# First attention: the addition of a group's sums moves from the end of its step on VectorE to behind the next step's first addition of counts

## The chip, the cores and the metric

One core of one Trainium2 chip runs the whole program. The time is the device time of one execution in microseconds; three runs of the kernel before gave 2632.73, 2643.93 and 2664.64 us. The profile is of one further execution. A core has the engines TensorE (PE, its weight loads PEld), VectorE (DVE), ScalarE (ACT), GpSimd (POOL) and SyncE (SP), which run their own instruction streams and wait for each other by semaphores.

## What is computed

A graph network of four layers over 3125 nodes and 100000 edges, the edges sorted by destination, each layer followed by a residual layer norm. The change touches the first layer, an attention with 4 heads of 16 features:

```python
score = (Kh[src] * Qh[dst] * (1.0 / np.sqrt(D)) * Ee).sum(-1)
score = jnp.exp(jnp.clip(score, -5.0, 5.0))
msg = Vh[src] * score[..., None]
wV = jax.ops.segment_sum(msg, dst, num_segments=n)
```

`Ee` is a linear map of 64 edge attributes. Beside it the same loop counts, for the second layer, how many edges go from each source to each destination.

## The kernel before, in words

The edges are worked in G = 98 groups of 1024 (128 partitions by C = 8 tiles). Every engine runs its own loop over the groups, unrolled by RS = 4, since the ring of gathered rows `kv`, of edge attributes `ea`, of indices `idx` and of query windows `qwin` has four slots. `j` counts sweeps over the edges; one sweep is run here.

GpSimd (L472 to L480) gathers keys and values of a group's sources by eight indirect DMAs (L476), one for each tile, into slot s of `kv`. After the fifth gather of a group it waits for the next group's indices, so it works in bursts: three gathers that finish one group and five of the next. SyncE (L423 to L433) waits on the semaphore `slot_free` until group g-4 is added, and then loads the indices (L338, 4 KB) and the edge attributes (L433, 256 KB) of group g.

VectorE's `step` (L627 to L673) for group g, in order: `prod` = edge products (bank 3, awaited by `ee_ok`) times gathered keys (L641); load of five registers of the group from `base_i` (L643: place `b` of the window of sums, and four places of the counts); times the query products (bank 4, `qd_ok`, L649); sum over the head's features (L651); clip (L653), which releases ScalarE's exponential; the first addition of counts (`add_counts(0)`, L635); the one-hot columns of the next group's nodes (`node_hots`, L613); the second addition of counts; the messages (L662, awaiting `ex_ok`); the third and fourth additions of counts; the key columns of the next group (`key_hots`, eight instructions at L620); and last the group's sums, bank 5 into `acc` (L672), awaiting `sum_ok`, with `slot_free` raised by it. That last one is what the change moves.

TensorE's `step` (L867 to L894): two of the four counts of the group (L875, two matmuls each; each waits for its bank by `bank_free`, raised by VectorE's additions), the turning of the next group's edge attributes (L833), the other two counts, the turning of its node columns (L841), the sums of the group (L890, awaiting `msg_ok`, raising `sum_ok`), and then the next group's edge products (L850, L852, raising `ee_ok`) and query products (L858, raising `qd_ok`).

ScalarE's `step` (L749 to L753): the exponential (L751), then for the next group: wait for `slot_free` of an earlier group, two loads of the query window (L733), copies of the turned edge attributes (L735) and node columns (L737), and the columns for the counts (L741, L747).

`pipelined` (L341 to L349) writes the loop: `front` of group 0, a hardware loop of 24 rounds of four steps from 0, and the last two groups behind it.

Of the kernel before, what the change touches and what calls it, by code (L numbers as in the profile page):

```python
# [8 lines left out]
ALU, ACT, AX = mybir.AluOpType, mybir.ActivationFunctionType, mybir.AxisListType  # L9

P = 128
N, D, E = 3125, 64, 100000
# [6 lines left out]
G = -(-E // ST)  # L19
PL = (E - (G - 1) * ST) // C  # L20
W = 64
# [3 lines left out]
GG = C // GT  # L25
# [3 lines left out]
RS = 4  # L29
# [37 lines left out]
def build(nc, x, src, dst, edge_attr_2, edge_attr_64, Wq, bq, Wk, bk, We, be, Wv, bv,  # L67
          attn_w, W_fc, W_attn, W_edge, W_e2n, W_m1, W_m2, out):
    ctx = ExitStack()
    with ctx:  # L70
# [50 lines left out]
        base_i = sb("base_i", [1, G, 8], i32)  # L121
# [252 lines left out]
        with nc.Block() as block:  # L374
# [115 lines left out]
            def _(dve):  # L490
# [115 lines left out]
                with dve.Fori(0, nj) as j:  # L606
                    dve.wait_ge(cleared, j + 1)
                    pass_on(dve)
                    start_sweep(dve, begun, True)

                    def node_hots(g, s, m):

                        nc.vector.tensor_tensor(hots[:, s % 2, :, :], bc(dst_rel[:, bass.ds(g, 1), :].rearrange("p g c -> p (g c)"), 2, W),  # L613
                                                bc(iota[:, 0:W], 1, C), ALU.is_equal).then_inc(hot_ok, 1)

                    def key_hots(g, s, m):

                        keys = tile_key[:, bass.ds(g, 1), :].rearrange("p g c -> p (g c)")
                        for c in range(C):
                            last = nc.vector.tensor_scalar(key_hot[:, c, :], iota_key[:, :], keys[:, c:c + 1], None, ALU.is_equal)  # L620
                        last.then_inc(key_ok, 1)

                    def front(g, s, m):
                        node_hots(g, s, m)
                        key_hots(g, s, m)

                    def step(g, s, m, after):  # L627

                        n = j * G + g + 1

                        def add_counts(q):

                            at = count[:, :, bass.ds(group_at[q], WC)]
                            dve.wait_ge(count_ok, j * (G * GG) + g * GG + q + 1)
                            nc.vector.tensor_tensor(at, at, bank[6 + q % 2][:, 0:KC].rearrange("p (h w) -> p h w", w=WC),  # L635
                                                    ALU.add).then_inc(bank_free, 1)

                        kvs = kv[:, s, :, :]
                        dve.wait_ge(kv_in[s], m * (16 * C))
                        dve.wait_ge(ee_ok, n)  # L640
                        nc.vector.tensor_tensor(prod[:, :].rearrange("p (c f) -> p c f", c=C),  # L641
                                                bank[3][:, :].rearrange("p (c f) -> p c f", c=C), kvs[:, :, 0:D], ALU.mult)
                        b, *group_at = nc.values_load_multi_w_load_instructions(  # L643
                            base_i[0:1, bass.ds(g, 1), 0:1 + GG].rearrange("a g k -> a (g k)"), engines=[mybir.EngineType.DVE],
                            min_val=0, max_val=NP,
                            skip_runtime_bounds_check_because="start_sweep keeps them within 0 and NP")[1]
                        dve.drain()
                        dve.wait_ge(qd_ok, n)
                        nc.vector.tensor_tensor(prod[:, :], prod[:, :], bank[4][:, :], ALU.mult)  # L649
                        dve.drain()  # L650
                        nc.vector.tensor_reduce(score[:, :], prod[:, :].rearrange("p (a d) -> p a d", d=DH), AX.X, ALU.add)  # L651
                        dve.drain()
                        nc.vector.tensor_scalar(score[:, :], score[:, :], -5.0, 5.0, ALU.max, ALU.min).then_inc(sc_ok, 1)  # L653

                        add_counts(0)
                        if after:

                            node_hots(*after)
                        dve.drain()
                        add_counts(1)  # L660
                        dve.wait_ge(ex_ok, n)
                        nc.vector.tensor_tensor(msg[:, :, 0:D].rearrange("p c (h d) -> p c h d", h=H),  # L662
                                                kvs[:, :, D:2 * D].rearrange("p c (h d) -> p c h d", h=H),
                                                bc(expo[:, :].rearrange("p (c h) -> p c h", h=H), 3, DH), ALU.mult).then_inc(msg_ok, 1)
                        for q in range(2, GG):
                            dve.drain()
                            add_counts(q)
                        if after:

                            key_hots(*after)  # L670
                        dve.wait_ge(sum_ok, n)
                        nc.vector.tensor_tensor(acc[0:D + 1, bass.ds(b, W)], acc[0:D + 1, bass.ds(b, W)], bank[5][0:D + 1, 0:W], ALU.add).then_inc(slot_free, 1)  # L672
                        dve.drain()  # L673

                    pipelined(dve, front, step)

            @block.scalar
            def _(act):
# [2501 lines left out]
```

## Time and the profile before

| | us |
|---|---|
| median of three runs | 2643.93 |
| the profiled execution | 2622.77 |
| its span, first to last instruction | 2621.0 |
| VectorE busy in the span | 1421.5 (54%) |
| GpSimd busy in the span | 1243.5 (47%) |
| TensorE matmuls busy in the span | 1481.0 (57%) |

A row of a group of instructions reads: line, engine, operation, out<-in, shapes, count | busy time in us, mean ns of one | idle time of the engine just before them in us, and what ended most of it. A row of a timeline reads: start in us from the span's start, duration in us, engine, line, operation, tiles, shape, count, and in brackets the idle time before it with what released it. "Issue" is time in which the engine waited for nothing that the profile shows; "remote" names no engine. Starts of matmuls are recorded, their ends are modelled. The first attention's loop runs from about 60 to 1466 us of the span.

### The profile page before, as it was taken

The page shows a single profiled execution, that of the slowest core. Times are in us where ns is not written, and L with a number is a line of the kernel's source. Part 1 is how long each engine was busy: PE and PEld are TensorE (multiplying, and loading weights), DVE is VectorE, ACT ScalarE, POOL GpSimd, SP SyncE. Part 2 cuts the span into 40 slices and gives each one's busy share as a digit, 9 for nine tenths or more (in the row PEclk, how much of TensorE's full clock was granted, in tenths as well). Part 3 has the DMA queues.
Part 4 walks back from the last instruction along what each step waited for, and adds up shares of the span by engine and source line. Part 5 has one row for each costly group of instructions (what it writes and reads, how often), then busy time and mean ns, then how long its engine had stood idle before and what let it go on. Part 6 is the DMA issues. An engine that isn't in the chain of part 4 may idle for free. (4 is left out here: it accounts for less than half of the span.)

```text
span 2621.0 us, 43664 instructions
## 1 busy us (share of the span) xinstructions
PE 1481.0 (57%) x12911; PEld 1234.8 (47%) x12911; DVE 1421.5 (54%) x3789; ACT 1011.9 (39%) x2229; POOL 1243.5 (47%) x1346
## 2 busy tenths in 40 slices
PE   4555555555555555555454586586103655556697
PEld 4444443434443443444343486475103645455586
DVE  6555554555555555555454787886202534344586
ACT  4333333333333333333233490591103533344575
POOL 5455555555555555555455191273764343444300
PEclk7777777777777777777777698696556777777898
DMA  4222222222222222222122120004111111111110
GB/s 130 52 58 58 56 59 54 60 57 57 58 58 58 55 59 58 58 57 56 52 59 55 39 67 22 1 2 125 35 24 25 36 34 38 34 42 32 35 34 14
DMA packets 112819, 128.69 MB, mean 49 GB/s; under 512 B 68447, under 2 KB 75923, under 8 KB 112426
## 3 DMA queue, kind: packets, MB, share of 16 engines
q0 software_dynamic: 35776, 62.74, 10.2%
q1 hardware_dynamic: 54842, 59.37, 7.8%
q10 hardware_dynamic: 22064, 4.85, 0.9%
q8 instruction: 75, 1.23, 0.2%
q14 instruction: 62, 0.51, 0.1%
HBM read 116.64 MB, written 10.20 MB: 48 GB/s over the span
## 5 line engine op out<-in xcount | busy, mean ns | idle before, releaser
L476 POOL DMA_INDIRECT shared<-kv_tab,idx x784 | 756.5, 965 | 668.0 <-DMA idx<-in_src 435.5
L875 PE MATMUL bank<-key_hot,lo_hot 128*128 128x350 f16 x784 | 218.7, 391 | 593.9 <-DVE count L635 399.1
L875 PEld LDWEIGHTS bank<-key_hot,lo_hot 128*128 128x128 f16 x784 | 57.5, 100 | 711.3 <-issue 699.2
L2455 POOL DMA_INDIRECT count<-att_tab,count x240 | 232.6, 969 | 261.4 <-PE bank L3009 156.0
L672 DVE TENSOR_TENSOR acc<-acc,bank 65x64 f32 x98 | 21.3, 218 | 486.2 <-remote 485.6
L751 ACT ACTIVATE expo<-score 128x32 f32<-128x32 f32 x98 | 22.5, 229 | 616.5 <-DVE score L653 609.9
L2837 ACT ACTIVATE shared<-shared 128x126 f32<-128x126 bf16 x336 | 143.6, 484 | 279.2 <-remote 175.6
L635 DVE TENSOR_TENSOR count<-count,bank 128x350 f32 x392 | 205.2, 523 | 81.6 <-issue 73.9
L741 ACT ACTIVATE lo_dist<-iota_neg,tile_lo 128x128 f16<-128x128 f32 x784 | 238.4, 390 | 0.0
L2986 PE MATMUL bank<-shared 128*128 128x150 f32 x896 | 156.7, 319 | 121.6 <-issue 56.2
L2986 PEld LDWEIGHTS bank<-shared 128*128 128x128 f32 x896 | 138.8, 208 | 146.2 <-issue 137.8
L620 DVE TENSOR_SCALAR key_hot<-iota_key,tile_key 128x350 f16<-128x350 f16 x784 | 192.3, 317 | 0.0
L890 PEld LDWEIGHTS bank<-hots,msg 128*65 128x65 f32 x1568 | 184.8, 222 | 0.4 <-DVE msg L662 0.4
L890 PE MATMUL bank<-hots,msg 128*65 128x64 f32 x1568 | 181.2, 304 | 0.0
L2952 PE MATMUL bank<-shared,ad_row 128*128 128x25 bf16 x1344 | 64.9, 177 | 205.5 <-issue 205.4
L2692 DVE TENSOR_TENSOR count<-count,bank 128x500 f32 x112 | 74.9, 668 | 167.6 <-remote 141.8
L2952 PEld LDWEIGHTS bank<-shared,ad_row 128*128 128x128 bf16 x1344 | 51.5, 99 | 216.2 <-issue 215.3
L850 PE MATMUL bank<-webd,eaT 128*128 128x128 f32 x784 | 144.0, 342 | 0.9 <-issue 0.9
L3020 PE MATMUL bank<-count,tab 128*68 128x88 f32 x1400 | 134.8, 265 | 8.4 <-DVE count L2692 6.5
L2455 POOL DMA_INDIRECT g_edge<-att_tab,count x94 | 88.9, 946 | 98.2 <-PE bank L3009 70.8
L3020 PEld LDWEIGHTS bank<-count,tab 128*68 128x68 f32 x1400 | 129.7, 162 | 12.2 <-DVE count L2692 8.6
L850 PEld LDWEIGHTS bank<-webd,eaT 128*128 128x128 f32 x784 | 132.4, 255 | 1.3 <-issue 1.3
(539 smaller groups left out, 3235.6 us busy)
## 6 DMA issues: line engine op xcount, KB each, us to landing
shared<-in_edge_attr SPq DMA_DIRECT2D x97, 256.0 KB
shared<-lo_tab SPq DMA_DIRECT2D x28, 512.0 KB
shared<-kv_tab,idx POOLq DMA_INDIRECT x784
count<-att_tab,count POOLq DMA_INDIRECT x240
qwin<-q_tab ACTq DMA_DIRECT2D x196, 16.0 KB
g_edge<-att_tab,count POOLq DMA_INDIRECT x94
idx<-in_src SPq DMA_DIRECT2D x93, 4.0 KB, 1.5
dh_tab<-acc SPq DMA_DIRECT2D x1, 1176.0 KB
```

The costliest lines, as they stand in the source:

```text
L476: nc.gpsimd.indirect_dma_start(kv[:, s, c, :], None, kv_tab, bass.IndirectOffsetOnAxis(ap=of[:, s, c:c + 1], axis=0)).then_inc(kv_in[s], 16)
L620: last = nc.vector.tensor_scalar(key_hot[:, c, :], iota_key[:, :], keys[:, c:c + 1], None, ALU.is_equal)
L635: nc.vector.tensor_tensor(at, at, bank[6 + q % 2][:, 0:KC].rearrange("p (h w) -> p h w", w=WC), ALU.add).then_inc(bank_free, 1)
L741: nc.scalar.activation(lo_dist[:, c, :], iota_neg[:, :], ACT.Abs, bias=los[:, c:c + 1])
L850: nc.tensor.matmul(bank[3][:, q * P:(q + 1) * P], eaT[:, q * P:(q + 1) * P], webd[:, :], start=q == 0, stop=False, skip_group_check=True)
L875: last = nc.tensor.matmul(bank[6 + q % 2][:, 0:KC], lo_hot[:, c, :], key_hot[:, c, :], start=i == 0, stop=i == GT - 1)
L890: last = nc.tensor.matmul(bank[5][0:D + 1, 0:W], msg[:, c, :], hots[:, s % 2, c, :], start=c == 0, stop=c == C - 1)
L2455: nc.gpsimd.indirect_dma_start(ring[s][:, j, 0:D + 2], None, att_tab[1], bass.IndirectOffsetOnAxis(ap=src_i[:, t:t + 1], axis=0)).then_inc ...
L2837: nc.scalar.activation(low_w[:, n % LOW_RING, 0:FREE], low_dist[:, n % LOW_RING, 0:FREE], ACT.Relu, bias=p, scale=minus_p).then_inc(low_ok, 1)
L2952: last = nc.tensor.matmul(bank[0][:, t * NT:(t + 1) * NT], lo_turned[:, s, t, :], u_parts[:, k, :], start=k == 0, stop=k == 2)
L2986: nc.tensor.matmul(into[:, 0:NT * QW].rearrange("p (h w) -> p h w", w=QW)[:, :, bass.ds(at[j], TW)], low_w[:, n % LOW_RING, :], keys_w[:, ...
L3020: last = nc.tensor.matmul(sum_of[0:D + 4, 0:UW], tab[:, h, 0:D + 4], blocks[:, i % 2, h, :], start=h == 0, stop=h == NT - 1, skip_group_ch ...
```

## The change

VectorE's stream alone is changed. `add_sums(g, s)` loads the window's place `b` by itself, waits for `sum_ok`, adds, and raises `slot_free`. It is called for group g-1 in the step of group g, behind `add_counts(0)`; the last group adds its own at the end of its step. The step's register load takes four registers in place of five. Since group 0 has none before it, the loop is written out: four steps peeled, then 23 rounds of four, then the last two.

```diff
+                    def add_sums(g, s):
+
+                        b = spans(dve, g)
+                        dve.wait_ge(sum_ok, j * G + g + 1)
+                        nc.vector.tensor_tensor(acc[0:D + 1, bass.ds(b, W)], acc[0:D + 1, bass.ds(b, W)], bank[5][0:D + 1, 0:W], ALU.add).then_inc(slot_free, 1)
+
                     def step(g, s, m, after):
 
                         n = j * G + g + 1
+                        first = isinstance(g, int) and g == 0
...
-                        b, *group_at = nc.values_load_multi_w_load_instructions(
-                            base_i[0:1, bass.ds(g, 1), 0:1 + GG].rearrange("a g k -> a (g k)"), engines=[mybir.EngineType.DVE],
+                        group_at = nc.values_load_multi_w_load_instructions(
+                            base_i[0:1, bass.ds(g, 1), 1:1 + GG].rearrange("a g k -> a (g k)"), engines=[mybir.EngineType.DVE],
...
                         add_counts(0)
+                        if not first:
+                            add_sums(g - 1, (s - 1) % RS)
                         if after:
 
                             node_hots(*after)
...
                             key_hots(*after)
-                        dve.wait_ge(sum_ok, n)
-                        nc.vector.tensor_tensor(acc[0:D + 1, bass.ds(b, W)], acc[0:D + 1, bass.ds(b, W)], bank[5][0:D + 1, 0:W], ALU.add).then_inc(slot_free, 1)
+                        else:
+                            add_sums(g, s)
                         dve.drain()
 
-                    pipelined(dve, front, step)
+                    front(0, 0, 1)
+                    for g in range(RS):
+                        step(g, g, 1, (g + 1, (g + 1) % RS, (g + 1) // RS + 1))
+                    with dve.Fori(1, G // RS) as it:
+                        for s in range(RS):
+                            step(it * RS + s, s, it + 1, (it * RS + s + 1, (s + 1) % RS, it + 1 + (s + 1) // RS))
+                    for g in range(G - G % RS, G):
+                        step(g, g % RS, g // RS + 1, (g + 1, (g + 1) % RS, (g + 1) // RS + 1) if g + 1 < G else None)
```

## Rows read from the trace of the kernel before

**Rows 1.** The page's costliest groups: GpSimd's gathers and the addition of the sums.
```profile
L476 POOL DMA_INDIRECT shared<-kv_tab,idx x784 | 756.5, 965 | 668.0 <-DMA idx<-in_src 435.5
...
L672 DVE TENSOR_TENSOR acc<-acc,bank 65x64 f32 x98 | 21.3, 218 | 486.2 <-remote 485.6
```

**Rows 2.** Who waited for whom, 60 to 1467 us: total us, times, longest us.
```profile
SPq L325 <- DVE acc L672: 1229.7, 93, 24.3
...
DVE acc L672 <- remote: 485.6, 93, 7.3
```

**Rows 3.** One group in order of time, all engines, 715 to 730 us.
```profile
715.27 0.22 DVE L672 TENSOR_TENSOR acc<-acc,bank 65x64 f32 x1 [4.83 <-remote]
715.68 0.69 DVE L641 TENSOR_TENSOR prod<-bank,shared 128x512 f32<-128x512 f32 x1 [0.19 <-issue]
...
716.47 0.69 DVE L649 TENSOR_TENSOR prod<-prod,bank 128x512 f32<-128x512 f32 x1
...
718.01 0.94 POOL L476 DMA_INDIRECT shared<-kv_tab,idx  x1 [4.49 <-DMA idx<-in_src]
...
718.27 0.52 DVE L635 TENSOR_TENSOR count<-count,bank 128x350 f32 x1
718.71 0.68 DVE L613 TENSOR_TENSOR hots<-dst_rel,iota 128x512 f32<-128x512 f32 x1
...
719.64 0.52 DVE L635 TENSOR_TENSOR count<-count,bank 128x350 f32 x1 [0.25 <-issue]
...
720.85 1.06 PE L841 MATMUL bank<-ident,hots 128*128 128x128 f32 x4
...
721.70 1.65 PE L890 MATMUL bank<-hots,msg 128*65 128x64 f32 x16
...
721.94 0.60 ACT L737 ACTIVATE hotT<-bank 128x512 f32<-128x512 f32 x1 [1.18 <-issue]
...
724.23 0.38 PE L852 MATMUL bank<-be_parts,ones_b 3*128 3x512 bf16 x1
...
724.55 1.16 PE L858 MATMUL bank<-qwin,hotT 128*128 128x128 f32 x8
...
726.68 0.76 PE L875 MATMUL bank<-key_hot,lo_hot 128*128 128x350 f16 x4 [0.98 <-ACT lo_hot L747]
726.95 0.94 POOL L476 DMA_INDIRECT shared<-kv_tab,idx  x1 [0.30 <-issue]
...
729.50 0.22 DVE L672 TENSOR_TENSOR acc<-acc,bank 65x64 f32 x1 [5.27 <-remote]
```

**Rows 4.** VectorE in order of time, 1230 to 1266 us.
```profile
1230.96 0.22 DVE L672 TENSOR_TENSOR acc<-acc,bank 65x64 f32 x1 [4.87 <-remote]
...
1242.14 0.22 DVE L672 TENSOR_TENSOR acc<-acc,bank 65x64 f32 x1 [2.22 <-remote]
1249.83 0.69 DVE L641 TENSOR_TENSOR prod<-bank,shared 128x512 f32<-128x512 f32 x1 [7.47 <-remote]
1257.52 0.69 DVE L649 TENSOR_TENSOR prod<-prod,bank 128x512 f32<-128x512 f32 x1 [7.00 <-remote]
...
1265.05 0.21 DVE L672 TENSOR_TENSOR acc<-acc,bank 65x64 f32 x1
```

**Rows 5.** GpSimd, first and last of sixteen gathers, 1230 to 1260 us.
```profile
1234.63 1.27 POOL L476 DMA_INDIRECT shared<-kv_tab,idx  x1 [5.44 <-DMA idx<-in_src]
...
1253.88 0.94 POOL L476 DMA_INDIRECT shared<-kv_tab,idx  x1 [0.30 <-issue]
```

**Rows 6.** TensorE's edge and query products in the same stretch.
```profile
1239.80 0.39 PE L852 MATMUL bank<-be_parts,ones_b 3*128 3x512 bf16 x1
1240.11 1.16 PE L858 MATMUL bank<-qwin,hotT 128*128 128x128 f32 x8
```

**Rows 7.** VectorE behind the last gather, 1448 to 1460 us.
```profile
1448.87 0.21 DVE L672 TENSOR_TENSOR acc<-acc,bank 65x64 f32 x1
...
1459.11 0.21 DVE L672 TENSOR_TENSOR acc<-acc,bank 65x64 f32 x1
```

## The prediction

> **What bounds the kernel now.** I read the page's costliest groups first, then who waited for whom, then one group in order of time. On the page GpSimd's gathers (L476, 784 of them) are the largest busy time, and nearly as long again idle, most of it until indices land; VectorE's addition of the sums (L672) has the longest idle time in front of it of all VectorE groups [rows 1]. The waits say the same as a ring: SyncE waits for L672 in 93 groups, and L672 waits 93 times, 485.6 us in all or 5.22 each, for something "remote" [rows 2]. "Remote" is put where the releasing semaphore moved long after the engine that should have moved it had ended.
>
> One group shows the ring closed [rows 3]. L672 at 715.27 frees the slot; the first gather of a burst of eight starts at 718.01 (2.74 later, the loads of indices between); the eighth starts at 726.95 and takes 0.94, so the burst lasts 9.88; the next L672 starts 1.61 after its end, at 729.50. 2.74 + 9.88 + 1.61 = 14.23 us, and that is the period. The point is the last term. The sums' products (L890) are drawn as ended at 721.70 + 1.65 = 723.35 and VectorE was through with the key columns at 724.23, but L672 starts at 729.50: after 5.27 of idle time, and 1.61 after the burst. So here a completion of TensorE that falls into a burst of gathers reaches VectorE only when the burst is over. Is it the sums' alone? Two groups in which GpSimd ran on without a pause answer it [rows 4 to 6]: a burst went from 1234.63 to 1254.82 (sixteen gathers), and there VectorE waited not only for the sums (1242.14) but then 7.47 us for the edge products (L641, whose last matmul L852 is drawn as ended at 1240.19) and 7.00 for the query products (L649; L858 ended at 1241.27). So the hold takes TensorE's later results too, and in a long burst lets them through one after another, over 7 us apart. In the common group they are late as well but behind L672: they cost nothing of their own. Without gathers, at the end, the period is 1459.11 - 1448.87 = 10.24 us [rows 7]: that is VectorE's and TensorE's own chain. GpSimd's least is eight gathers at the step of that burst, 8 x (726.95 - 718.01) / 7 = 10.2 us.
>
> When does the hold begin? In rows 3 the transposes L841, drawn to 720.85 + 1.06 = 721.91, 3.9 us into the burst, were in time (ScalarE's copy L737 follows at 721.94), the sums, drawn to 5.3 us in, were not.
>
> The Trainium skill says otherwise ("SBUF - State Buffer", Who interferes with whom): DMA never contends with a compute engine, and only VectorE and GpSimd can block each other, at the shared port. By that rule the gathers cannot be what holds TensorE's results; the rows above go against it, and what it would make of the time is the last rival.
>
> **The change part by part.**
> 1. *The wait leaves the end of the step.* From group 0 on VectorE goes from L620 straight to L641. Removed there: L672's 0.22 and its issue gap, 715.68 - 715.27 = 0.41 [rows 3]. Late next is L641's own input, the edge products. In the present cadence they are not released before the sums, so at this place the change alone gains 0.41 at most.
> 2. *The sums are added behind the first count.* L641 to the first L635 is 718.27 - 715.68 = 2.59 [rows 3]. Behind L635 comes L672 at a spacing of at least 0.44 (L613 followed so), plus the register load of the window's place, which now stands here. The trace of before has no such load in this position: between 0 (hidden under L635's 0.52) and about 0.25 (the issue gap ahead of the second L635, 719.64, where a register is worked out behind a drain). I take 0.60 from L635 to L672. L613 and everything behind it comes later by about as much: 0.60 against 0.44 and L672's 0.22, say 0.5 to 0.6.
> 3. *What is queued behind it.* The slot is freed by L672, so SyncE's two loads and GpSimd's burst move with it: 2.59 + 0.60 = 3.19 us later against L641, 3.34 behind the first count. ScalarE waits for slots of three groups earlier and is not reached. No DMA is added; their order is the same.
> 4. *The peeled first four groups* and the last addition: more code, run once; a microsecond or two, unseen.
>
> Now the results of TensorE against the new burst. Taken from rows 3, counted from the first L635 (718.27) and 0.60 later than now, the burst starting at 3.34: sums end at 5.08 + 0.60 = 5.68, that is 2.3 into the burst; edge products (724.61) at 6.94, 3.6 in; query products (725.71) at 8.04, 4.7 in; the first counts (727.44) at 9.77, 6.4 in. The hold began between 3.9 and 5.3 in. So sums and edge products would pass, the query products stand on the edge and the counts behind it. I take the query products as held: the sixteen matmuls of the sums, within which the hold began in rows 3, now lie in the burst's first 2.3 us, and should bring it on no later than they did. Then L649 starts where L672 started before, 1.61 after the burst, and the new period is
> 1.61 + (L649 to first L635, 718.27 - 716.47 = 1.80) + 0.60 + 2.74 + 9.88 = 16.63 us, 2.40 more.
> If the edge products are held too, L641 is the one released and it is 1.61 + 2.59 + 0.60 + 2.74 + 9.88 = 17.42, 3.19 more. The two groups of the long burst, where exactly these products were held, took 1265.05 - 1230.96 = 34.09, 17.05 each [rows 4]: between the two.
> Of 93 waits of L672 two belong to that odd pair; 91 periods x 2.40 = +218 us. The profiled execution took 2622.8 us around a span of 2621.0; the median of the runs is 2643.9, 0.8% above it. On the execution the sum gives 2841, on the median 2862. The spread of the three runs is 1.2%, so about 1% is what a measurement can tell from no change.
>
> **The rivals.**
> *Only the counts are held (0.14).* The query products pass, the counts don't: 1.61 + 0.60 + 2.74 + 9.88 = 14.83, +0.60 x 91 = +55: 2699. For it: 4.7 lies in a window of 3.9 to 5.3. Against: with the products in time and a few counts let through one by one, the slot comes free inside the burst, which then runs on as in rows 5.
> *Only the sums are late (0.08).* Then L641 and L649 go ahead, VectorE stands at L672 behind the first count, and it is released where it is now: 1.61 + 2.74 + 9.88, the ring is the same, +0: 2644. It would also mean that the change removes a wait and finds it again a few instructions on. Against it: rows 4, where L641 and L649 wait 7 us each.
> *The burst comes too late to hold anything that matters (0.22), the faster side.* The slot is freed later, the burst starts later against TensorE's work; if the hold begins more than 4.7 us into a burst for the query products, and more than 6.4 for the counts, then the next step starts unheld. The bound is the tail's 10.24 [rows 7] or GpSimd's 10.2. But the slots then come free while a burst runs, GpSimd no longer pauses, and rows 4 and 5 show what an unbroken burst costs. Half of the way from 14.23 to 10.24, 2.0 x 91 = -182: 2462. It decides at 4.7 us: hold later than that, faster; earlier, slower.
> *No hold by gathers at all (0.06).* The wait of L672 would be the sums' own delay of some other cause, covered by the new place; the period is that of the tail, 3.99 x 91 = -363: 2281. Rows 4 speak against it, and the idle time of L672, which is there only while gathers run (rows 7 have none). By the rule of the Trainium skill cited above this is the case to expect.
>
> **How the numbers follow.** Forecast 0.50: 2862, its own range 2750 (products let through after part of the burst) to 2950 (edge products held: 2644 + 290 = 2934). Slower by over 1%: 0.50 and 0.10 of the first rival, 0.60. Within 1%: 0.04 of it and 0.08, 0.12. Faster by over 1%: 0.22 + 0.06 = 0.28. The range for eight in ten reaches from 2400, past the faster rival's 2462, to 2950; left out are the last rival and some 0.05 on either side.
>
> **What would show it.** Right: L672 directly behind the first L635 with next to no idle time; the idle time of 5.2 us has moved to L649 (or L641), "remote"; the bursts still of eight gathers with a pause, the pause longer than now (about 6.8 us against 14.23 - 9.88 = 4.35), the period 16.6 to 17.4; SyncE still waiting for L672 in every group. Wrong: L672 waits at its new place and the period is 14.2 (sums alone); or L641, L649 and L672 all without idle time and a period near 10 to 12 (the faster side); or bursts of sixteen, short and long groups in turn, which would give a mean I can't place better than between the cases.

## The result, and the profile after the change

The changed kernel takes 2879.5 us (median of 4 runs, 2871.7 to 2892.3) against 2654.3 for the kernel before in the same measurement (4 runs, 2632.7 to 2665.6). The ratio is 1.086, with a 95% interval of 1.077 to 1.096: slower. The forecast was 2862 with a range of 2750 to 2950, and the measured time lies 17 above the one and inside the other. Every time in us below is read from one profiled execution of its kernel; that of e2 took 2801.7 us, slower than its other four runs (2743.6 to 2755.5).

The profiled execution took 2885.2 us (span 2883.4). Its page, the groups that answer to [rows 1]:

```profile
L476 POOL DMA_INDIRECT shared<-kv_tab,idx x784 | 752.8, 960 | 911.3 <-DMA idx<-in_src 676.8
...
L648 DVE TENSOR_TENSOR prod<-bank,shared 128x512 f32<-128x512 f32 x98 | 67.8, 692 | 557.8 <-remote 510.7
...
L656 DVE TENSOR_TENSOR prod<-prod,bank 128x512 f32<-128x512 f32 x98 | 67.5, 688 | 231.7 <-remote 229.6
```

The gathers cost what they did (752.8 us busy against 756.5), but GpSimd stands idle in front of them for 911.3 us instead of 668.0. The addition of the sums (now L631) is not among the costliest groups any more. The idle time marked "remote" now stands ahead of the edge products' multiplication (L648) and the query products' (L656), 740.3 us together against the 485.6 of the sums before. The waits, 60 to 1750 us (us in total, times, longest), beside [rows 2]:

```profile
SPq L325 <- DVE acc L631: 1447.1, 92, 27.4
POOL shared L476 <- DMA idx<-in_src: 676.8, 94, 18.6
DVE prod L648 <- remote: 510.7, 87, 8.7
DVE prod L656 <- remote: 229.6, 95, 5.7
```

One group in order of time, all engines, 711 to 732 us (start, duration, engine, line; idle time before in brackets), beside [rows 3]:

```profile
711.85 0.22 DVE L631 TENSOR_TENSOR acc<-acc,bank 65x64 f32 x1
...
714.81 0.95 POOL L476 DMA_INDIRECT shared<-kv_tab,idx  x1 [7.04 <-DMA idx<-in_src]
715.00 1.96 PE L906 MATMUL bank<-hots,msg 128*65 128x64 f32 x16
...
717.93 0.38 PE L868 MATMUL bank<-be_parts,ones_b 3*128 3x512 bf16 x1
718.24 1.16 PE L874 MATMUL bank<-qwin,hotT 128*128 128x128 f32 x8
...
723.46 0.69 DVE L648 TENSOR_TENSOR prod<-bank,shared 128x512 f32<-128x512 f32 x1 [6.07 <-remote]
723.65 0.94 POOL L476 DMA_INDIRECT shared<-kv_tab,idx  x1 [0.30 <-issue]
726.34 0.69 DVE L656 TENSOR_TENSOR prod<-prod,bank 128x512 f32<-128x512 f32 x1 [2.19 <-remote]
...
728.15 0.53 DVE L642 TENSOR_TENSOR count<-count,bank 128x350 f32 x1
728.71 0.22 DVE L631 TENSOR_TENSOR acc<-acc,bank 65x64 f32 x1
...
731.77 0.95 POOL L476 DMA_INDIRECT shared<-kv_tab,idx  x1 [7.17 <-DMA idx<-in_src]
```

Read it as a ring again. The addition at 711.85 frees the slot; the burst starts at 714.81 (2.96 later) and its eighth gather ends at 723.65 + 0.94 = 724.59 (9.78); the query products, drawn as ended at 718.24 + 1.16 = 719.40, reach VectorE at 726.34 (1.75 behind the burst); 1.81 to the first count, 0.56 to the addition. 2.96 + 9.78 + 1.75 + 1.81 + 0.56 = 16.86 us. The addition itself has no idle time before it, as the prediction asked for; the bursts are still of eight gathers (93 of the 95), the pause between them is 7.04 and 7.17 us here against the 6.8 forecast, and SyncE still waits for the addition, 92 times. TensorE's own speed is not in this ring: its granted clock in the group was 0.70 against 0.77 from 700 to 730 us before, but the query products are drawn as ended 6.94 us before VectorE gets them. Over the whole stage the first and the last of the 98 additions start at 93.20 and 1706.90, 16.64 us a group; before it was 82.96 and 1466.11, 14.26 a group. So the last addition comes 240.8 us later. The two spans differ by 262.4; the other 21.6 us lie behind the stage (2883.4 - 1706.9 = 1176.5 us against 1154.9). They are scatter: in e3 and e8 below, which have the same code there, that part took 1153.9 and 1148.2, and in e1 1179.0.

### The profile page after: what moved, and what is told of

Same layout as the page of the kernel before. It is cut to its first block and busy times, and to the rows that moved or that the text cites. A ratio compares the mean times of both kernels' runs of the same rounds, so it can differ in the third digit from the quotient of the medians.

```text
span 2883.4 us, 43835 instructions
## 1 busy us (share of the span) xinstructions
PE 1531.2 (53%) x12911; PEld 1292.2 (45%) x12911; DVE 1415.4 (49%) x3789; ACT 1013.4 (35%) x2229; POOL 1237.9 (43%) x1346
## 5 line engine op out<-in xcount | busy, mean ns | idle before, releaser
L476 POOL DMA_INDIRECT shared<-kv_tab,idx x784 | 752.8, 960 | 911.3 <-DMA idx<-in_src 676.8
L891 PE MATMUL bank<-key_hot,lo_hot 128*128 128x350 f16 x784 | 225.1, 401 | 823.6 <-DVE count L642 799.0
L648 DVE TENSOR_TENSOR prod<-bank,shared 128x512 f32<-128x512 f32 x98 | 67.8, 692 | 557.8 <-remote 510.7
L906 PEld LDWEIGHTS bank<-hots,msg 128*65 128x65 f32 x1568 | 192.4, 230 | 0.4 <-DVE msg L671 0.4
L906 PE MATMUL bank<-hots,msg 128*65 128x64 f32 x1568 | 189.8, 313 | 0.0
L656 DVE TENSOR_TENSOR prod<-prod,bank 128x512 f32<-128x512 f32 x98 | 67.5, 688 | 231.7 <-remote 229.6
L866 PE MATMUL bank<-webd,eaT 128*128 128x128 f32 x784 | 167.8, 382 | 0.9 <-issue 0.9
L866 PEld LDWEIGHTS bank<-webd,eaT 128*128 128x128 f32 x784 | 154.4, 292 | 1.3 <-issue 1.3
```

The costliest lines, as they stand in the source:

```text
L476: nc.gpsimd.indirect_dma_start(kv[:, s, c, :], None, kv_tab, bass.IndirectOffsetOnAxis(ap=of[:, s, c:c + 1], axis=0)).then_inc(kv_in[s], 16)
L866: nc.tensor.matmul(bank[3][:, q * P:(q + 1) * P], eaT[:, q * P:(q + 1) * P], webd[:, :], start=q == 0, stop=False, skip_group_check=True)
L891: last = nc.tensor.matmul(bank[6 + q % 2][:, 0:KC], lo_hot[:, c, :], key_hot[:, c, :], start=i == 0, stop=i == GT - 1)
L906: last = nc.tensor.matmul(bank[5][0:D + 1, 0:W], msg[:, c, :], hots[:, s % 2, c, :], start=c == 0, stop=c == C - 1)
```

## The experiments

Twelve kernels ran. Each is compared by its ratio to the kernel before in the same measurement, because the kernel before took 2608 to 2614 us there and not 2654. "Period" is the time from the first to the last of the 98 additions of sums in the kernel's own trace, divided by 97.

| Run | What is different | Ratio (95% interval) | Period, us |
|---|---|---|---|
| kernel before | | 1 | 14.26 |
| changed kernel | | 1.086 (1.077 to 1.096) | 16.64 |
| e1 | written-out loop, sums at end | 0.994 (0.990 to 0.998) | 13.82 |
| e2 | slot freed behind messages | 1.054 (1.052 to 1.056) | 15.66 |
| e3 | slot freed at end of step | 1.098 (1.094 to 1.103) | 16.57 |
| e4 | changed, 4 gathers | 0.923 (0.918 to 0.927) | 12.05 |
| e5 | changed, plain loads | 0.839 (0.832 to 0.845) | 9.91 |
| e6 | before, sums of 2 tiles | 1.067 (1.059 to 1.075) | 15.95 |
| e7 | before, waits for 5 and 3 | 0.992 (0.988 to 0.996) | 13.89 |
| e8 | changed, waits for 5 and 3 | 1.087 (1.078 to 1.095) | 16.24 |
| e9 | before, plain loads | 0.811 (0.806 to 0.816) | 9.14 |
| e10 | before, 4 gathers | 0.822 (0.815 to 0.829) | 9.38 |
| e11 | before, burst started by TensorE's sums | 0.931 (0.923 to 0.938) | 12.25 |
| e12 | before, pause after every 4 gathers | 1.008 (1.004 to 1.012) | 14.45 |

### e1: the written-out loop alone

```diff
                         add_counts(0)
-                        if not first:
-                            add_sums(g - 1, (s - 1) % RS)
...
                             key_hots(*after)
-                        else:
-                            add_sums(g, s)
+                        add_sums(g, s)
```

> The loop written out as in the changed kernel, the sums still added at the end of the step (with the register load that the new function brings). Theory (the place of the addition makes the difference, by way of the slot that it frees): the ring is that of before, one group every 14.2 us, ratio to the kernel before 0.99 to 1.01. Rival (the written-out code or the second register load costs something by itself): some part of the 0.086, so a ratio over 1.02.

Measured: 2602.3 us, ratio 0.994 (0.990 to 0.998). As the theory said; the loop written out and the second register load cost nothing, and if anything give 12 us back. By the traces it is 13.82 us a group against 14.26, so against this kernel the place of the addition costs 2.82 us a group and not 2.38. What follows is about that place.

### e2 and e3: another instruction frees the slot

Both keep the sums where the changed kernel has them and take the semaphore from the addition. e2 gives it to the drain behind the messages, e3 to the last drain of the step.

```diff
-  ... bank[5][0:D + 1, 0:W], ALU.add).then_inc(slot_free, 1)
+  ... bank[5][0:D + 1, 0:W], ALU.add)
...
                         for q in range(2, GG):
-                            dve.drain()
+                            d = dve.drain()
+                            if q == 2:
+                                d.then_inc(slot_free, 1)
```

> The changed kernel, but the slot is freed by the first drain behind the messages and no longer by the addition of sums. The burst of gathers then starts some 6 us behind the first count instead of 3.5. Theory (what counts is which of TensorE's results fall late into the burst): edge and query products of the next group fall 1 to 2.5 us into the burst and go through, the later counts or the sums are held; the idle time leaves the edge and query products, and the period falls below 16.9, to 14 to 16 us: ratio to the kernel before 0.99 to 1.07. Rival 1 (each microsecond by which the slot is freed later makes the period one microsecond longer, whatever falls where): 16.9 + 2.6 = 19.5 us, ratio near 1.17. Rival 2 (the place of the addition matters by itself, not the slot): 16.9 us as in the changed kernel, ratio 1.09.

> The changed kernel, but the slot is freed by the drain at the end of the step, some 6 us behind the first count, so the burst starts some 8.7 us behind it. Theory: next group's products and its first count lie ahead of the burst or early in it and go through; what is late in the burst are that group's messages' counts and sums, and the slot of the next group comes free while the burst still runs, so bursts run into each other. Between the kernel before and the changed one: period 14 to 17 us, ratio 0.99 to 1.09. Rival 1 (one microsecond of slot is one of period): 16.9 + 5.4 = 22.3 us, ratio about 1.27. Rival 2 (place of the addition by itself): ratio 1.09.

Measured: e2 2753.7 us, ratio 1.054; e3 2861.5 us, ratio 1.098 (1.094 to 1.103), a little above the theory's 1.09. e2 frees the slot later than the changed kernel and is faster all the same: that refutes "a microsecond of slot is a microsecond of period" as well as "the place of the addition by itself". e3 is far from that rival's 1.27. A stretch of e2 in order of time, all engines:

```profile
807.21 0.69 DVE L648 TENSOR_TENSOR prod<-bank,shared 128x512 f32<-128x512 f32 x1 [11.64 <-remote]
...
815.60 1.07 POOL L476 DMA_INDIRECT shared<-kv_tab,idx  x1 [11.37 <-DMA idx<-in_src]
...
817.33 0.69 DVE L648 TENSOR_TENSOR prod<-bank,shared 128x512 f32<-128x512 f32 x1 [1.03 <-PE bank L870]
...
822.61 0.46 PE L893 MATMUL bank<-key_hot,lo_hot 128*128 128x350 f16 x2 [1.20 <-DVE count L642]
822.93 1.08 PE L859 MATMUL bank<-ident,hots 128*128 128x128 f32 x4
...
824.13 0.52 DVE L642 TENSOR_TENSOR count<-count,bank 128x350 f32 x1 [0.25 <-issue]
...
828.42 0.60 ACT L755 ACTIVATE hotT<-bank 128x512 f32<-128x512 f32 x1 [5.46 <-remote]
...
830.51 0.37 PE L876 MATMUL bank<-qwin,hotT 128*128 128x128 f32 x1 [0.24 <-issue]
...
832.64 0.37 PE L876 MATMUL bank<-qwin,hotT 128*128 128x128 f32 x1 [1.76 <-issue]
...
838.54 0.69 DVE L648 TENSOR_TENSOR prod<-bank,shared 128x512 f32<-128x512 f32 x1 [11.96 <-remote]
```

The groups come in pairs. In the first the products (817.33) lie 1.7 us into the burst and go through. So does all of that group's work up to its last count: TensorE's (L893) is drawn as ended 7.5 us into the burst, and VectorE adds it at 824.13 without a "remote" wait. Then the slot comes free inside the burst, GpSimd runs on, and the next group is caught: the transposes drawn to 822.93 + 1.08 = 824.01 reach ScalarE's copy at 828.42, TensorE's own instructions go out one every 2.1 us (830.51, 832.64), and the edge products arrive at 838.54 after 11.96 us of idle time. The pair takes 838.54 - 807.21 = 31.3 us. So e2's ratio came as its theory said, but the idle time left the edge products only in every second group: 478.4 us "remote" at L648 are left, in 47 waits. e3 has such pairs too, slower: its L648 stands idle 14.66 us "remote" (829.59) and 1.39 us (840.30) in turn. Its bursts here are of eight with 1.24 us between two of them, and that gap (816.56 to 817.79) did not let the edge products through, which are drawn as ended at 815.79. This is the pattern that the prediction named for bursts of sixteen, and what it gave as the case against its faster rival [rows 4, 5].

### e4 and e10: half the gathers, in both orders

```diff
                        for c in range(C):
-                            nc.gpsimd.indirect_dma_start(
+                            if c < C // 2:
+                              nc.gpsimd.indirect_dma_start(
...
-                        dve.wait_ge(kv_in[s], m * (16 * C))
+                        dve.wait_ge(s_const, 5)
+                        dve.wait_ge(kv_in[s], m * (16 * C // 2))
```

`s_const` is raised once, ahead of the stage, when GpSimd has filled the other half of the slots with zeros.

> The changed kernel with four gathers in a group instead of eight: the key and value rows of tiles 4 to 7 are left out (zeros in their place), everything else stands. The burst lasts about 4.9 us instead of 9.8. Theory (the gathers hold TensorE's completions till the burst is over): either nothing is held, and the period is VectorE's own, 10.2 to 10.6 us, or the query products, drawn 4.6 us into the burst, are held to 1.75 behind it: 1.75 + 1.81 + 0.56 + 2.96 + 4.9 = 12.0 us. 2880 - 91 x 4.9 = 2435 or, without any hold, 2290 us; ratio to the kernel before 0.86 to 0.92. Rival (TensorE's results are late for a reason that has nothing to do with gathers): idle time ahead of the products stays, period 16.9 or little less, ratio over 1.05.

> The kernel before with four gathers in a group instead of eight, as in e4 (key and value rows of tiles 4 to 7 left out). Burst from 2.7 to 7.7 us behind the addition of sums. Theory: the sums are drawn as ended 8.1 us behind it, after the burst, so nothing is held that matters, and the period is VectorE's own, 10.2 to 10.5 us against 12.2 in e4: ratio 0.85 to 0.87, e4 0.06 to 0.07 slower than this. Rival (the later addition hurts by other ways than the hold, or the hold catches counts here): period over 11 us, ratio over 0.88.

Measured: e4 2403.1 us, ratio 0.923; e10 2142.8 us, ratio 0.822. e4 in order of time, VectorE and GpSimd:

```profile
808.27 0.22 DVE L633 TENSOR_TENSOR acc<-acc,bank 65x64 f32 x1
...
811.20 0.95 POOL L478 DMA_INDIRECT shared<-kv_tab,idx  x1 [7.43 <-DMA idx<-in_src]
...
815.03 0.94 POOL L478 DMA_INDIRECT shared<-kv_tab,idx  x1 [0.30 <-issue]
...
816.92 0.69 DVE L651 TENSOR_TENSOR prod<-bank,shared 128x512 f32<-128x512 f32 x1 [3.01 <-remote]
...
820.43 0.22 DVE L633 TENSOR_TENSOR acc<-acc,bank 65x64 f32 x1
```

With the burst 5 us shorter the wait moves with its end: released 0.95 us behind the last gather (816.92 against 815.97), group 12.2 us, where the theory's held case said 12.0. That the two lie so close is partly luck: the theory had the query products held, to 1.75 behind the burst, and here it is the edge products, to 0.95, with 2.95 us from them to the first count and not 1.81. In 30 of the 98 groups the same wait ends on the edge products without a "remote". In e10 nothing is held, and one group follows the other in 8.9 to 9.4 us. The ratios of the two orders differ by 0.923 - 0.822 = 0.10. That is more than the 0.06 to 0.07 I had expected, because e10 is faster than the 10.2 us that I had taken for VectorE's own chain.

### e5 and e9: no gathers, plain loads of the same bytes

```diff
+                        for c in range(C):
+                            sp.dma_start(kv[:, s, c, :], kv_tab[c * P:(c + 1) * P, :]).then_inc(kv_in[s], 16)
...
-                            nc.gpsimd.indirect_dma_start(
-                                kv[:, s, c, :], None, kv_tab, bass.IndirectOffsetOnAxis(ap=of[:, s, c:c + 1], axis=0)
-                            ).then_inc(kv_in[s], 16)
```

> The changed kernel without gathers: SyncE loads eight blocks of 128 consecutive rows of the key and value table into the same places of the slot, the same number of bytes and of rows; the rows are not those that the edges name, so the attention is computed from other keys and values. GpSimd has nothing left to do in the stage. Theory (GpSimd's gathers hold TensorE's completions): nothing is held, the period is VectorE's and TensorE's own of 10.2 to 10.6 us, the kernel near 2270 to 2320 us, ratio to the kernel before 0.86 to 0.88. Rival (it is the traffic into SBUF, whoever issues it): results late in the load are still released behind its end, idle time marked remote ahead of the products, period over 11.5 us, ratio over 0.91.

> The kernel before with the plain loads of e5 in place of its gathers (the key and value rows are again not those of the edges). With e5 it makes the fourth corner: both places of the addition, with gathers and without. Theory (the place of the addition costs only through the gathers that it starts): the same as e5 within 1%, period 10.0 to 10.3 us, ratio to the kernel before 0.83 to 0.85. Rival (the two places differ by themselves): the later place saves a wait or costs one without gathers too, over 1% between the two; the part of it that is the changed kernel's 0.086 would show as a ratio near 0.77 here.

Measured: e5 2197.0 us, ratio 0.839; e9 2118.8 us, ratio 0.811. The same stretch of VectorE's addition in e5 and then in e9:

```profile
799.87 0.22 DVE L633 TENSOR_TENSOR acc<-acc,bank 65x64 f32 x1
...
809.93 0.22 DVE L633 TENSOR_TENSOR acc<-acc,bank 65x64 f32 x1
```

```profile
800.75 0.21 DVE L674 TENSOR_TENSOR acc<-acc,bank 65x64 f32 x1
...
810.06 0.21 DVE L674 TENSOR_TENSOR acc<-acc,bank 65x64 f32 x1
```

In neither does VectorE wait once for anything "remote" in this stage. The changed kernel falls from 16.64 to 9.91 us a group: it is the gathers, and not the 0.5 MB of traffic into the same slot, that hold TensorE's results. But the theory's "same within 1%" fell. The changed order takes 0.839 / 0.811 = 1.034 times as long even here, 0.77 us a group. In e9 the addition stands behind the key columns, while TensorE works on sums and edge products; in e5 it stands ahead of the messages (VectorE from L650 to L673: 811.45 - 806.41 = 5.04 us; in e9 from L643 to L664 806.14 - 801.70 = 4.44), on which TensorE's sums wait, and these on which the next edge products. That is 0.60 us here and 0.64 in the mean of the stage; half of the 0.64 is the addition, the other 0.31 a longer way from the edge products' multiplication to the query products', where VectorE waits for TensorE (0.47 us ahead of L658 in this group of e5). For the rest there is the granted clock of TensorE, in the stretch from 200 to 700 us (busy time of the engines, then PEclk, DMA share, GB/s; e5, then e9):

```profile
200.00:700.00 500.00, 351.38 (x2459) 277.09 (x2457) 379.99 (x956) 245.37 (x601) 0.00 (x0) 0.87 0.30 82
```

```profile
200.00:700.00 500.00, 347.50 (x2679) 265.58 (x2678) 405.31 (x1040) 268.60 (x659) 0.00 (x0) 0.93 0.33 90
```

0.87 against 0.93. Whether the lower clock is cause or effect of the longer group these runs don't tell.

Is it TensorE's code that comes late, fetched behind the gathers? Between 200 and 1200 us of the changed kernel's trace the instruction queues moved 4 packets in all, in some sixty groups, nearly all of which were held: no.

### e6: fewer of TensorE's instructions

```diff
-                        for c in range(C):
-                            last = nc.tensor.matmul(bank[5][0:D + 1, 0:W], msg[:, c, :], hots[:, s % 2, c, :], start=c == 0, stop=c == C - 1)
+                        for c in range(2):
+                            last = nc.tensor.matmul(bank[5][0:D + 1, 0:W], msg[:, c, :], hots[:, s % 2, c, :], start=c == 0, stop=c == 1)
```

> The kernel before, the sums of a group taken over two of its eight tiles: 4 of TensorE's 16 instructions of the sums are left, and the sums of the other six tiles are left out. Everything else stands. In e2 TensorE's results passed until 8 us into a burst and the hold began with the sums again, so it may come from the number of TensorE's instructions, the sums' being the densest run of them. Theory A (the hold builds up with TensorE's instructions inside a burst): with 12 fewer the sums pass, and of what follows perhaps the edge and query products too; the wait of the sums' addition falls from 5 us to under 1, and the period to 10.5 to 12.5 us, ratio 0.87 to 0.94. Theory B (it begins a fixed time into the burst, 4 to 5 us): the sums, ended 1.2 us earlier, may pass, but edge and query products at 5.0 and 6.1 us in are held; their wait takes the place of the sums', period 14 to 17 us, ratio 0.99 to 1.09.

Measured: 2787.2 us, ratio 1.067 (1.059 to 1.075). Theory A's forecast (0.87 to 0.94) fell, theory B's time came; a build-up by TensorE's instructions is not excluded by that, since the edge products bring their own. VectorE, e6:

```profile
810.48 0.20 DVE L672 TENSOR_TENSOR acc<-acc,bank 65x64 f32 x1
...
822.89 0.69 DVE L641 TENSOR_TENSOR prod<-bank,shared 128x512 f32<-128x512 f32 x1 [12.22 <-remote]
825.75 0.69 DVE L649 TENSOR_TENSOR prod<-prod,bank 128x512 f32<-128x512 f32 x1 [2.16 <-remote]
```

With the sums smaller, they are through in time (no idle time at 810.48), the slot comes free inside the burst, the next burst joins on, and the edge products wait 12.22 us. GpSimd in the same stretch, the first and last of sixteen gathers:

```profile
802.98 0.94 POOL L476 DMA_INDIRECT shared<-kv_tab,idx  x1 [12.89 <-DMA idx<-in_src]
...
822.02 0.94 POOL L476 DMA_INDIRECT shared<-kv_tab,idx  x1 [0.30 <-issue]
```

To take TensorE work away made the kernel 7% slower: this is the trap of the faster rival, by another door.

### e7 and e8: two waits meant to split the burst

```diff
                         for c in range(C):
+                            if g >= RS and c in (0, 5):
+                                pool.wait_ge(qd_ok if c == 0 else sum_ok, j * G + g - 2)
+                                pass_on(pool)
                             nc.gpsimd.indirect_dma_start(
```

> The kernel before, with each group's gathers in two bursts: gathers 0 to 4 wait until TensorE has given the query products of three groups before, gathers 5 to 7 until it has given that group's sums. e4 showed results released 0.95 us behind the last of four gathers. Theory (a pause in the gathers lets through what is held): from query products to sums 5 x 1.25 + 0.95 = 7.2 us, from sums to the next query products 3 x 1.25 + 0.95 = 4.7 us, period 11.9 to 12.9 us: 2614 - 91 x (14.2 - 12.4) = 2450, ratio to the kernel before 0.91 to 0.95. Rival (the hold lasts as long as any gather is queued, or the two waits cost more than they give): 14.2 us or more, ratio 1.00 to 1.10.

> The same two bursts in the changed kernel. Theory (the place of the addition hurts only by the place of the burst that it starts): the slot is asked for long after it came free, so both orders of VectorE give the same within 0.3 us a group, ratio 0.91 to 0.95. Rival (the later addition costs by itself): its 2.6 us a group remain, ratio 0.09 above that of e7.

Measured: e7 2594.7 us, ratio 0.992; e8 2835.5 us, ratio 1.087. Neither the gain nor the equality of the orders. The two kernels are what e1 and the changed kernel were, and the traces show why: GpSimd still runs bursts of eight (in e7 805.77 to 816.18) and still waits for indices, 392.3 us in 93 waits (e1: 371.1 in 94). My waits were the last to pass once at most (2.3 us "remote" in e7, 0.3 in e8). The code puts the wait for the next group's indices ahead of gather 5 of a group, so a burst is gathers 5 to 7 of one group and 0 to 4 of the next, and both begin only when the same sums have freed a slot. A flaw of the experiment; it says nothing on pauses. e12 and e11 put it right.

### e11: TensorE's sums start the burst

```diff
                         for c in range(C):
+                            if c == 5 and g >= RS - 1:
+                                pool.wait_ge(sum_ok, j * G + g - 2)
+                                pass_on(pool)
                             nc.gpsimd.indirect_dma_start(
...
-                            if c == C // 2 and RS <= g + 1 < G:
+                            if c == C - 1 and RS <= g + 1 < G:
                                 indices(g + 1)
```

> The kernel before; a burst of eight is started by TensorE's completion of the sums itself: gathers 5 to 7 of a group, whose slot is long free, wait for it, and only gathers 0 to 4 of the next group wait for the indices, which land meanwhile. That takes the 2.7 us between the addition and the first gather out of the ring. Theory, if the transposes and counts still pass, now 2.5 us later in the burst: 9.9 + 1.6 + 0.3 = 11.8 us, ratio 0.91 to 0.93. Rival (they are held too, as the hold in e2 and e3 began between 5 and 8 us into a burst and in the kernel before between 4 and 5): their work comes behind the burst, 14 us or more, ratio 0.99 to 1.10.

Measured: 2428.6 us, ratio 0.931 (0.923 to 0.938): faster than both kernels, by 7% and 14%. All engines, in order of time:

```profile
802.30 0.22 DVE L675 TENSOR_TENSOR acc<-acc,bank 65x64 f32 x1 [3.16 <-remote]
802.94 0.94 POOL L479 DMA_INDIRECT shared<-kv_tab,idx  x1 [2.40 <-remote]
...
807.87 1.06 PE L844 MATMUL bank<-ident,hots 128*128 128x128 f32 x4
...
808.97 0.60 ACT L740 ACTIVATE hotT<-bank 128x512 f32<-128x512 f32 x1 [1.21 <-issue]
...
811.77 0.94 POOL L479 DMA_INDIRECT shared<-kv_tab,idx  x1 [0.30 <-issue]
...
814.55 0.22 DVE L675 TENSOR_TENSOR acc<-acc,bank 65x64 f32 x1 [3.23 <-remote]
```

The ring is the one of [rows 3] without the way over VectorE, SyncE and the indices: 0.64 (802.30 to the first gather) + 9.77 (the burst, to 812.71) + 1.84 (the release) = 12.25 us. The rival fell: though the burst now starts 2.1 us earlier against everything, transposes (drawn as ended 6.0 us into the burst, copied by ScalarE at 808.97) and counts pass, and from 132 us on VectorE's "remote" waits are for the sums alone, 188.5 us in all. GpSimd waits "remote" for the same sums, 239.1 us in 93 waits: their completion is late for both engines.

### e12: a pause after every fourth gather

```diff
                             ).then_inc(kv_in[s], 16)
...
+                            if c in (C // 2 - 1, C - 1):
+                                pool.wait_ge(kv_in[s], (g // RS * C + c + 1) * 16)
+                                pass_on(pool)
```

> The kernel before; behind every fourth gather GpSimd waits until the four have landed, some 2 us. Theory (a pause of 1 us or more releases what is held, e4's was 0.95 us): GpSimd needs 2 x (5.0 + 1.7 to 2.0) = 13.4 to 14.0 us a group, no result is held for over 5 us, and with slots three groups ahead this is the period: ratio 0.97 to 1.00. Rival (the hold goes on through such a pause, as if the burst were 14 us long): 2.74 + 13.7 + 1.6 = 18.0 us, ratio near 1.13.

Measured: 2633.8 us, ratio 1.008 (1.004 to 1.012). Its waits, 60 to 1700 us:

```profile
DVE prod L644 <- DMA shared<-kv_tab,idx: 567.5, 94, 7.3
POOL shared L476 <- DMA shared<-kv_tab,idx: 449.2, 192, 3.0
```

Of VectorE's "remote" waits in the stage one of 2.6 us is left, and now it waits for the rows themselves. GpSimd, e12, and the sums of one group:

```profile
802.10 0.94 POOL L476 DMA_INDIRECT shared<-kv_tab,idx  x1 [2.42 <-DMA shared<-kv_tab,idx]
...
807.47 1.96 PE L893 MATMUL bank<-hots,msg 128*65 128x64 f32 x16
...
809.64 1.02 POOL L476 DMA_INDIRECT shared<-kv_tab,idx  x1 [2.29 <-DMA shared<-kv_tab,idx]
809.77 0.21 DVE L675 TENSOR_TENSOR acc<-acc,bank 65x64 f32 x1
...
816.80 0.94 POOL L476 DMA_INDIRECT shared<-kv_tab,idx  x1 [2.39 <-DMA shared<-kv_tab,idx]
```

816.80 - 802.10 = 14.7 us a group in this stretch: a pause is 2.3 to 2.4 us and not the 1.7 to 2.0 I gave it, and two of them eat what the missing hold gives, so that the ratio ends just above the 0.97 to 1.00 of the theory. The rival's 18.0 us fell: the sums, drawn as ended in the pause at 809.43, 7.3 us behind the first gather, are added at 809.77. Of the edge and query products the run says less. They end inside the next four gathers, and VectorE waits until 816.24 for the rows, 1.8 us behind the last of these: a hold of 0.95 us, as in e4, would not be seen.

## Why the prediction was right, point by point

*The ring and its sum.* 16.63 was forecast, 16.86 measured. Term by term: release behind the burst 1.61, measured 1.75; L649 (now L656) to the first count 1.80, measured 1.81; first count to addition 0.60, measured 0.56; addition to first gather 2.74, measured 2.96; burst 9.88, measured 9.78. The largest miss is the way from the addition to the gathers. Over the stage, 2.38 us a group more were measured against 2.40 forecast, and the two medians differ by 225 us against 218. So close a match of the mean is in part luck: the group above is 2.63 us longer than the one of [rows 3], and against e1 the mean is 2.82. The figure of 2862 is 17 below the result; 10 of these are the kernel before itself, 2654.3 in this measurement and 2643.9 in the one shown.

*Step 1, the wait leaves the end of the step.* Right, and nothing else gained by it.

*Step 2, the spacing of 0.60.* Right in size. It was read only as a shift of the slot. e5 and e9 show that it is also work ahead of the messages that used to lie beside TensorE's sums: without gathers it would cost some 3% by itself. In the ring of the changed kernel it is counted once, as the 0.56.

*Step 4, the written-out loop at nothing.* Right (e1, 0.994): it cost nothing.

*Which results are held.* Here a step failed, without harm to the sum. The text let the edge products pass, 3.6 us into the burst, since the hold began "between 3.9 and 5.3". They were drawn as ended at 718.31, 3.5 us in, and reached VectorE at 723.46, 8.65 in. Their hold ended inside the burst and the query products' 1.75 behind it, so only the latter sets the period. For the same reason the text's second case, 17.42 with L641 released behind the burst, did not come either. The error was to read an onset in microseconds from one group. In e2 the counts passed up to 7.5 us into a burst, in the changed kernel the edge products did not at 3.5. The onset is no fixed time. The text's own reason for the query products, that the sixteen matmuls of the sums bring the hold on, fits here, where the sums lie in the burst's first 2.2 us; but e6, with four of the sixteen, still held the edge products, and no run isolates it.

*The hold itself.* Shown to be the gathers' doing: half of them, and the release moves with the burst's end (e4); a pause after four, and VectorE no longer waits for TensorE (e12); plain loads of as many bytes, and it is gone (e5, e9). What is argued only is the means by which it acts. The late transposes in e2, GpSimd's late start in e11 and TensorE's instructions at one every 2.1 us in e2 show that it is not the semaphore on its way to VectorE alone. The term "release behind the burst" is not a constant either, though the sum took it as one: in the median 0.97 us behind four gathers (e4), 1.67 and 1.75 behind eight (before, changed), 2.97 behind sixteen (e2). Gathers of fewer bytes, and GpSimd work of the same length without any DMA, were not tried, so whether the building of descriptors or their transfer does it stays open.

*The rivals.* Sums alone late, counts alone held, no hold: all refuted by the trace after, where L648 and L656 wait 740 us. By the rule of the last of these, that of the Trainium skill ("SBUF - State Buffer", Who interferes with whom), DMA never contends with a compute engine. e5 and e9 agree with it for plain loads, at 9.91 and 9.14 us a group; with the gathers the same stage takes 16.64 and 14.26, and there the measurement decides against it. The faster rival, a burst too late to hold anything, was built as e2 and e3: the products of one group do get through, and the joined burst takes it back from the next, as the text said against it. The bound given with these rivals was wrong: 10.24 us a group, from the tail [rows 7], is not the least, for e9 needs 9.14 and e10 9.38. In the tail's group TensorE was slow: it had stood idle for 8.95 us, from 1440 to 1450 us its granted clock was 0.50, the lower of its two levels (1.2 GHz), and VectorE waited 1.47 us for the edge products (L641, 1450.55). In e9 the mean clock from 200 to 700 us was 0.93. The place for the faster side was elsewhere than any rival had it: not a later burst but an earlier one (e11).

## What to carry to other kernels

Before moving an instruction, list what its semaphore starts, and ask what the started work will lie beside: here moving a 0.2 us addition cost 2.4 us a group, because the burst of GpSimd gathers that it starts moved onto TensorE's products, and VectorE's way from the query products to the addition (1.81 + 0.56 us) came into the ring. Where results arrive "remote" a microsecond or two behind a burst of gathers, the time to win is in the way from the last of these results to the next burst; let TensorE's own semaphore start gathers whose slot is long free, and wait for the indices only ahead of the gather that reads them (e11, 7% faster than the kernel before). And place small VectorE work where VectorE waits for TensorE anyway, not ahead of what TensorE waits for.

## What the runs showed of the hardware that I had not expected

- Gathers issued by GpSimd delay TensorE's results, plain loads into the same buffer do not: 16.64 against 9.91 us a group with the same eight blocks of 64 KB.
- A pause of 2.3 us after four gathers is enough that VectorE waits for no result of TensorE (e12); a gap of 1.24 us between eight and eight was not (e3). Behind four gathers results came at 0.95 us, behind eight at 1.6 to 2.0 (1.84 and in the median 2.00 in e11), behind sixteen at 2.97.
- How long a burst may run before it holds anything differs: 3.5 us were too long for the edge products in the changed kernel, 7.5 us were not for the counts in e2, whose burst came after 11.4 us without gathers against 7.0. The length of that stretch does not settle it: in e11, after 2.4 us without gathers, the transposes passed 6.0 us into the burst.
- Less TensorE work can make the kernel slower: e6 dropped 12 of 16 instructions of the sums and lost 7%, by joining two bursts.
